# Edge keys for duplicate detection: broadcast by TensorE passes, or stored to DRAM and read back as broadcast rows

## The chip, the cores and the metric

One core of one Trainium2 chip runs the whole program. The metric is the device time of one execution in microseconds (us), as a median over runs. The engines are TensorE (PE: matmuls, and PEld: its weight loads), VectorE (DVE), ScalarE (ACT), GpSimd (POOL) and SyncE (SP), which here only issues DMAs. ScalarE and GpSimd issue DMAs too. 16 DMA engines carry the transfers of all of them.

## What is computed

The reference runs a two-layer graph network on 384 tokens of width 1024 and 12288 edges. Only the first layer's graph attention touches the edges in the part at issue:

```python
def _build_mask(edge_index, edge_type, edge_type_weights, dtype):
    src, dst = (edge_index[0], edge_index[1])
    w = jax.nn.softplus(edge_type_weights)
    mask = jnp.full((N, N), -jnp.inf, dtype=dtype)
    mask = mask.at[src, dst].set(w[edge_type - 1])     # the last edge of a (src, dst) pair wins
    ...
q = x @ wq.T + bq; k = x @ wk.T + bk; v = x @ wv.T + bv
q2, k2, v2 = second projections, 16 heads of 64
scores = einsum('hnd,hmd->hnm', q2, k2) * scale + mask[None]
out = softmax(scores) @ v2, then @ wo.T + bo
x = x + _L0_gnn_ref(xn, ...) + _L0_mix_ref(xn, ...)    # then expert layers, and layer 1
```

Layer 1 sums over the same edges and needs for each (dst, src) pair how many edges it has.

## The kernel before

**Projections on TensorE.** Six first projections of xn (three for each of two branches) are called layers 0 to 5 (`layer_A`). Each takes eight weight chunks of 512 KB from a ring of eight slots (`ring`). `chunk_T` multiplies one chunk, 8 matmuls of 384 columns, into bank 0 or 1, and ScalarE evicts it (L633). Two second projections follow (L658 evicts them), then V2 (`chunk_N`, L886) in two halves, between whose chunks the first score matmuls (L966) are written. The third score group waits until VectorE has read the first one, and VectorE reads scores only with the finished mask (L1486).

**Weights.** SyncE refills a slot each time its chunk has been used (`load`, L360).

**Edges.** 12288 edges are 96 columns of 128. An edge's key is 384 src + dst. GpSimd makes the key of each edge in a column (`keyf`) and its transpose key (`rkeyf`). To find duplicates inside a column, every partition needs all 128 keys of that column as a row. TensorE makes these rows (`keys(layer)`, L912 and L913): for each of 16 columns in a layer, two accumulating fp16 matmuls against scaled identities, into banks 4 to 7. It does so ahead of each of the six layers. VectorE's `dedup` (L1410) compares each row, read from PSUM, with its own key and counts later duplicates. It then makes scatter addresses (`kidx`, `ridx`) and counts (L1415 to L1420).

**Scatters on GpSimd.** GpSimd first fills four tables in DRAM (w_lo, w_hi, n_lo, n_hi: 576 KB each, with a tail of 0.5 KB; L471, L472). When all have landed it scatters column after column: 48 turns of four indirect DMAs (`put`, L453). A put waits for the one before it into the same table. Each group of 8 turns also waits for `spots_ready` of the dedup for one layer. Then it reads the tables back (L486), and VectorE combines them to the mask (L1464 to L1473), which the score stage needs.

**ScalarE's queue** loads the edges and constants first, and after the input transposes the two bias rows bo_g and bo_m, broadcast into `rows` (L616, L617), the gate weights wqkv and the centroids cent. GpSimd adds the two bias rows after its table reads (L496).

Of the kernel before, what the change touches and what calls it, by code (L numbers as in the profile page):

```python
# [29 lines left out]
P = 128  # L30
N = 384
# [125 lines left out]

def program(nc, x, stream, c32, c16, cols_d, edges_d, up0_d, dn0_d, wqkv_d, cent_d,
            bo_g, bo_m, a_lr, gam_d, bet_d, b2_d,
            xs, ys, yo, w_lo, w_hi, n_lo, n_hi, out):  # L160
    with ExitStack() as ctx:
        def sb(name, shape, dt=F32):
            return ctx.enter_context(nc.sbuf_tensor(name, shape, dt))

        def sem(name):
            return ctx.enter_context(nc.semaphore(name))
# [28 lines left out]
        ridx = sb("ridx", [P, ET], U32)  # L195
        src16 = sb("src16", [P, ET], F16)
        dst16 = sb("dst16", [P, ET], F16)
        wqkv = sb("wqkv", [P, KB, 3 * NE])
# [29 lines left out]
        iota = k16[:, 0:384]  # L228
        id16 = k16[:, 384:512]
        id384 = k16[:, 512:640]  # L230
        token = k16[:, 640:643]

# [40 lines left out]
        edges_ready = sem("edges_ready")  # L273
        keys_ready = sem("keys_ready")
        sp_in = sem("sp_in")
        sp_out = sem("sp_out")
# [37 lines left out]


        junk = CT[:].rearrange("p b n -> p (b n)").bitcast(BF16)[:, 0:GT_ * P].rearrange("p (t n) -> p t n", t=GT_)
        tmp = [G[:, i * 3072:(i + 1) * 3072] for i in range(3)]
# [37 lines left out]
        def _(sp):  # L355
# [3 lines left out]
            def load(r, c):  # L359
                sp.dma_start(ring[:, r, :], stream[c]).then_inc(landed[r], 16)  # L360

            for r in range(SLOTS):
                load(r, r)
            with sp.Fori(1, CH_L1 // 8) as g:
                for r in range(SLOTS):
                    sp.wait_ge(chunk_used, 8 * g - 7 + r)
                    load(r, 8 * g + r)

# [78 lines left out]
        def _(pool):  # L447
# [9 lines left out]
            step(pool.memset(none, 0.0))  # L457
            pool.wait_ge(edge_in, 16)
            pool.tensor_copy(src16[:], ed[:, 0, :])
            pool.tensor_copy(dst16[:], ed[:, 1, :]).then_inc(edges_ready, 1)  # L460
            pool.tensor_copy(srcf[:], ed[:, 0, :])
# [4 lines left out]
            pool.tensor_tensor(keyf[:], keyf[:], dstf[:], ALU.add)  # L466
            pool.tensor_tensor(rkeyf[:], rkeyf[:], srcf[:], ALU.add).then_inc(edges_ready, 1)
            pool.wait_ge(x_in[NB - 1], 16)
# [105 lines left out]
        def _(act):  # L574
            step = Chain(act, astep)
            act.dma_start(ed[:], edges_d).then_inc(edge_in, 16)
            act.dma_start(cols[:], cols_d).then_inc(k_in, 16)
# [8 lines left out]
            def seed(c):  # L586

                act.wait_ge(var_ready, c + 1)
                act.activation(lnv[:], ve[:], ACT.Sqrt).then_inc(rstd_seed, 1)
# [15 lines left out]
            step(act.activation(spw[:, 0, :], cols[:, C_EW:C_EW + 4], ACT.Copy))  # L605
            act.activation(spw[:, 2, :], spw[:, 1, :], ACT.Exp, scale=-1.0).then_inc(beta_exp, 1)
            seed(0)
            for b in range(NB):
# [6 lines left out]
            act.activation(spw[:, 1, :], spw[:, 3, :], ACT.Ln).then_inc(act_output, 1)  # L615
            act.dma_start(rows[:, 0, :], bo_g.to_broadcast([P, D])).then_inc(biases_and_gates_in, 16)  # L616
            act.dma_start(rows[:, 1, :], bo_m.to_broadcast([P, D])).then_inc(biases_and_gates_in, 16)  # L617
            act.dma_start(wqkv[:], wqkv_d).then_inc(biases_and_gates_in, 16)
# [33 lines left out]


            act.wait_ge(mixs_ready, 8)
            with act.Fori(0, 2) as j:
# [203 lines left out]
        def _(pe):  # L859
# [45 lines left out]

            def keys(layer):
                pe.wait_ge(edges_ready, 2 * layer + 2)
                for g in range(2):
                    for t in range(GT_):
                        dst = bank[4 + 2 * g + t // 4][:, (t % 4) * P:(t % 4 + 1) * P]  # L910
                        e = (layer + HG * g) * 8 + t
                        pe.matmul(dst, src16[:, bass.ds(e, 1)].to_broadcast([P, P]), id384, start=True, stop=False)  # L912
                        last = pe.matmul(dst, dst16[:, bass.ds(e, 1)].to_broadcast([P, P]), id16,  # L913
                                         start=False, stop=True)
                    last.then_inc(keys_ready, 1)

            pe.wait_ge(k_in, 48)
            keys(0)
            for b in range(NB):
# [11 lines left out]
            def layer_A(layer, before=None):  # L931
                if not isinstance(layer, int) or layer:
                    keys(layer)
                for m in range(KB):
                    if before:
                        before(m)
                    chunk_T(m, lambda k: xnT[:, k, :], layer * 8 + m + T_A - 1, layer * 16 + 16, m % 2)

            layer_A(0)
            with pe.Fori(1, 5) as layer:  # L940
                layer_A(layer)
# [58 lines left out]
            pe.wait_ge(mixs_taken, 8)  # L1000
            pe.wait_ge(edges_ready, 2 + EG)
            for kk in range(4):
# [337 lines left out]
        def _(v):  # L1340
# [62 lines left out]
            def dedup(layer, q):  # L1403

                group, turn_ = layer + HG * q, layer * 2 + q
                v.wait_ge(keys_ready, turn_ + 1)
                for t in range(GT_):
                    e = group * 8 + t
                    src = bank[4 + 2 * q + t // 4][:, (t % 4) * P:(t % 4 + 1) * P]
                    last = stt(junk[:, t, :], src, keyf[:, bass.ds(e, 1)], same, ALU.is_equal, ALU.mult,  # L1410
                               accum_out=ndup[:, bass.ds(e, 1)])
                last.then_inc(edges_ready, 1)
                v.wait_ge(edges_ready, turn_ + 3)
                g8 = bass.ds(group * 8, GT_)
                ts(count[:, g8], ndup[:, g8], 256.0, None, ALU.mult)  # L1415
                step(ts(lastf[:], ndup[:, g8], 1.0, None, ALU.is_lt))
                stt(spot[:, 0, :], keyf[:, g8], beyond, lastf[:], ALU.subtract, ALU.mult)
                step(stt(spot[:, 1, :], rkeyf[:, g8], beyond, lastf[:], ALU.subtract, ALU.mult))
                ts(kidx[:, g8], spot[:, 0, :], beyond, None, ALU.add)
                ts(ridx[:, g8], spot[:, 1, :], beyond, None, ALU.add).then_inc(spots_ready, 1)  # L1420
                v.wait_ge(spots_ready, turn_ + 1)
# [476 lines left out]
def constants():  # L1898
# [11 lines left out]
    token = np.arange(N).reshape(NB, P).T  # L1910
    c16 = np.concatenate([np.tile(np.arange(N), (P, 1)), ident, ident * N, token], 1).astype(np.float16)
    return c32, c16
# [42 lines left out]
```

## Time and profile before

| | us |
|---|---|
| median of 3 runs (1207.18 to 1212.54) | 1211.57 |
| the profiled execution, its own time | 1217.39 |
| its span in the trace | 1215.4 |
| PE busy | 1032.0 (85%) |
| DVE busy | 337.9 (28%) |
| ACT busy | 211.0 (17%) |
| POOL busy | 321.7 (26%) |

The times of this table are one execution's, apart from the median. All positions below are us from the start of its span. A share of busy time is a mean over very different stages: TensorE is busy in most of them, yet the chain of work that ended last gives 22% of the span to GpSimd. What ends each wait is to be read in the stage itself.

### The profile page before, as it was taken

The numbers are of one execution on the slowest core, as the hardware profiler recorded it, in microseconds if no ns is written. First come the engines' busy times: TensorE is split into PE (matmuls) and PEld (weight loads), VectorE is DVE, ScalarE is ACT, GpSimd is POOL, SyncE is SP. The second block draws the span as 40 slices with busy tenths as digits, with TensorE's granted clock in tenths as the row PEclk, the third lists the DMA queues.
The fourth block names the chain that finished last, engine by engine and source line by source line (L and its number), as shares of the span: only waits on it lengthen the run. The fifth ranks groups of instructions, "written<-read, shape, count | busy, mean of one in ns | idle before, by whom it ended". The sixth has DMA issues, their size and how long they took to land.

```text
span 1215.4 us, 10270 instructions
## 1 busy us (share of the span) xinstructions
PE 1032.0 (85%) x3516; PEld 562.9 (46%) x3516; DVE 337.9 (28%) x911; ACT 211.0 (17%) x443; POOL 321.7 (26%) x250
## 2 busy tenths in 40 slices
PE   6999999999999787999479997299999999357553
PEld 4566656655554344444455563144445554242210
DVE  5036332271000566110431010402204541820002
ACT  3122311111111366100111111101101000114100
POOL 3088888888888100000000000100000000002000
PEclk9999999999999899999679999599999999559777
DMA  9964544444446200122448983722230223436786
GB/s 276 165 111 95 104 92 99 92 99 88 104 104 166 102 1 1 56 85 92 147 142 296 352 325 118 272 98 98 99 104 18 87 81 96 169 111 236 284 300 246
DMA packets 62251, 170.44 MB, mean 140 GB/s; under 512 B 22144, under 2 KB 22656, under 8 KB 62080
## 3 DMA queue, kind: packets, MB, share of 16 engines
q1 hardware_dynamic: 36832, 140.53, 35.6%
q0 software_dynamic: 21632, 17.94, 8.8%
q10 hardware_dynamic: 3744, 11.42, 2.5%
q8 instruction: 24, 0.39, 0.1%
q14 instruction: 19, 0.16, 0.0%
HBM read 156.39 MB, written 13.47 MB: 140 GB/s over the span
## 4 chain that ended last, share of the span: by engine, by line
PE 49%; POOL 22%; DMA 11%; issue 8%; DVE 7%; ACT 2%; SPq 1%; ACTq 0%; DVEq 0%; POOLq 0%
PE bank L886 20%; POOL n_hi L453 7%; PE bank L1093 6%; POOL n_lo L453 6%; POOL w_hi L453 4%; POOL w_lo L453 4%; PE bank L875 3%; DMA n_hi<-G 3%; PE bank L1118 3%; PE bank L1300 2%; DMA ring<-in_stream 2%; PE bank L1318 2%; PE bank L995 1%; PE bank L981 1%; PE bank L1231 1%
## 5 line engine op out<-in xcount | busy, mean ns | idle before, releaser
L875 PE MATMUL bank<-xnT,ring 128*128 128x384 f32 x896 | 292.7, 487 | 1.5 <-ACT xnT L612 1.0
L875 PEld LDWEIGHTS bank<-xnT,ring 128*128 128x128 f32 x896 | 169.7, 190 | 119.6 <-ACT xnT L612 1.2
L506 POOL DMA_INDIRECT Y<-xs,idx x12 | 12.3, 1025 | 624.4 <-DVE idx L1603 509.5
L886 PE MATMUL bank<-ring,Y 128*128 128x512 f32 x384 | 168.5, 599 | 0.8 <-DVE Y L1820 0.8
L886 PE MATMUL bank<-ring,xnT 128*128 128x512 f32 x288 | 124.0, 592 | 0.6 <-ACT xnT L597 0.6
L886 PEld LDWEIGHTS bank<-ring,Y 128*128 128x128 f32 x384 | 73.3, 192 | 94.7 <-issue 92.5
L453 POOL DMA_INDIRECT n_hi<-count,ridx x48 | 84.4, 1758 | 14.6 <-issue 14.0
L886 PEld LDWEIGHTS bank<-ring,xnT 128*128 128x128 f32 x288 | 54.6, 190 | 68.7 <-issue 67.9
L453 POOL DMA_INDIRECT n_lo<-count,ridx x48 | 81.8, 1704 | 14.6 <-issue 14.3
L875 PE MATMUL bank<-Y,ring 128*128 x256 | 82.7, 486 | 0.0
L1093 PE MATMUL bank<-ring,Y 128*128 128x352 f32 x256 | 79.1, 468 | 0.7 <-issue 0.7
L1300 PE MATMUL bank<-ring,Y 128*64 128x512 f32 x128 | 37.3, 742 | 39.2 <-DMA ring<-in_stream 31.0
L633 ACT ACTIVATE Y<-bank,sbias,scale 128x384 f32 (+1 forms) x48 | 32.2, 671 | 214.0 <-PE bank L875 214.0
L867 PE MATMUL bank<-k,xn 128*128 128x128 f32 x72 | 17.1, 412 | 59.7 <-DVE xn L1369 58.3
L453 POOL DMA_INDIRECT w_lo<-wts,kidx x48 | 51.7, 1077 | 55.3 <-DMA n_hi<-G 40.9
L875 PEld LDWEIGHTS bank<-Y,ring 128*128 128x128 f32 x256 | 48.6, 190 | 33.9
L1093 PEld LDWEIGHTS bank<-ring,Y 128*128 128x128 f32 x256 | 49.1, 194 | 27.4 <-issue 2.6
L453 POOL DMA_INDIRECT w_hi<-wts,kidx x48 | 51.8, 1078 | 14.6 <-issue 14.6
L1410 DVE SCALAR_TENSOR_TENSOR CT<-bank,keyf,k 128x128 bf16<-128x128 f32 x96 | 27.0, 347 | 66.0 <-PE bank L913 64.6
L506 POOL DMA_INDIRECT Y<-ys,idx x9 | 8.5, 947 | 138.1 <-DMA ys<-Y 136.0
L867 PEld LDWEIGHTS bank<-k,xn 128*128 128x128 f32 x72 | 12.2, 209 | 66.4 <-DVE xn L1369 60.8
L1300 PEld LDWEIGHTS bank<-ring,Y 128*64 128x64 f32 x128 | 11.6, 169 | 62.6 <-issue 58.3
(252 smaller groups left out, 972.2 us busy)
## 6 DMA issues: line engine op xcount, KB each, us to landing
ring<-in_stream SPq DMA_DIRECT2D x160, 512.0 KB, 3.7
ring<-in_up SPq DMA_DIRECT2D x32, 704.0 KB, 5.6
G<-in_stream SPq DMA_DIRECT2D x32, 512.0 KB, 7.1
ring<-in_dn SPq DMA_DIRECT2D x7, 1024.0 KB, 5.8
ys<-Y ACTq DMA_DIRECT2D x12, 512.0 KB, 7.6
Y<-in_dn SPq DMA_DIRECT2D x7, 384.0 KB, 6.8
Y<-in_b SPq DMA_DIRECT2D x8, 256.0 KB, 11.1
xr<-in_x SPq DMA_DIRECT2D x3, 512.0 KB, 4.9
```

Source lines behind the costliest of these rows:

```text
L453: pool.indirect_dma_start(table, bass.IndirectOffsetOnAxis(ap=at[:, e:e + 1], axis=0), what[:, e:e + 1], None, **how).then_inc(done, 16)
L506: pool.indirect_dma_start(dst, None, src, bass.IndirectOffsetOnAxis(ap=idx[:, col:col + 1], axis=0))\
L633: act.activation(dst, bank[m % 2][:, 0:N], ACT.Identity, bias=bi, scale=sc).then_inc(t_evicted, 1)
L867: last = pe.transpose(bank[n % 2][:, b * P:(b + 1) * P], src[:, b, m * P:(m + 1) * P], ident)
L875: last = pe.matmul(bank[to][:, 0:N], ring[:, r, k * P:(k + 1) * P], rhs(k), start=(k == 0), stop=(k == KB - 1))
L886: last = pe.matmul(bank[2 + 3 * half + b][:], lhs(k0 + k, b), ring[:, r, k * 512:(k + 1) * 512], start=(start and k == 0), stop=(stop and ...
L981: last = pe.transpose(bank[4 + mb][:, b * P:(b + 1) * P], S[:, u, b, mb * P:(mb + 1) * P], ident)
L1093: last = pe.matmul(bank[2 + h][:, 0:F0], x_, W[:, o:o + F0], **se)
L1118: last = pe.matmul(bank[5 + half][:], h_, w_, start=(f == 0), stop=(f == 2))
L1300: last = pe.matmul(bank[2][a * HC:(a + 1) * HC, :], XgT[i % 2][:, 2 * j + k, a * HC:(a + 1) * HC], ringf[:, o:o + 512], start=(j == 0 and ...
L1318: last = pe.matmul(bank[5 + half][a * HC:(a + 1) * HC, :], hT[:, 2 * kk + k, a * HC:(a + 1) * HC], G[:, o:o + 512], start=(kk == 0 and k = ...
L1410: last = stt(junk[:, t, :], src, keyf[:, bass.ds(e, 1)], same, ALU.is_equal, ALU.mult, accum_out=ndup[:, bass.ds(e, 1)])
```

## The change

The program no longer makes the key rows on TensorE. The edges come in a second layout too (`edge_rows`, 96 partitions of 128 src and 128 dst, lying in `mask` until the mask is made). GpSimd makes a table of keys from it, 96 x 128, and ScalarE stores that to DRAM (`keys_d`, 48 KB), ahead of its first square root. SyncE then reads 8 columns at a time back, broadcast to 128 partitions, into `rows`: two reads of 512 KB for each layer, the first pair behind the eight first ring loads, the others in the middle of the layer before. VectorE's comparison reads `rows` in SBUF in place of PSUM. Since `rows` is in use, the two bias rows are loaded after layer 5. The fp16 constants and `src16`, `dst16` go.

```diff
@@ SyncE
             for r in range(SLOTS):
                 load(r, r)
-            with sp.Fori(1, CH_L1 // 8) as g:
+            def load_keys(layer):
+                for q in range(2):
+                    sp.dma_start(rows[:, q, :].rearrange("p (t n) -> p t n", t=GT_),
+                                 keys_d[bass.ds((layer + HG * q) * GT_, GT_), :].unsqueeze(0)
+                                 .to_broadcast([P, GT_, P])).then_inc(key_rows_in, 16)
+            def next_chunk(g, r):
+                sp.wait_ge(chunk_used, 8 * g - 7 + r)
+                load(r, 8 * g + r)
+            sp.wait_ge(keys_stored, 16)
+            load_keys(0)
+            with sp.Fori(1, HG) as g:
                 for r in range(SLOTS):
-                    sp.wait_ge(chunk_used, 8 * g - 7 + r)
-                    load(r, 8 * g + r)
+                    next_chunk(g, r)
+                    if r == 3:
+                        sp.wait_ge(edges_ready, 2 * g + 2)
+                        load_keys(g)
@@ GpSimd
-            pool.wait_ge(edge_in, 16)
-            pool.tensor_copy(src16[:], ed[:, 0, :])
-            pool.tensor_copy(dst16[:], ed[:, 1, :]).then_inc(edges_ready, 1)
+            pool.wait_ge(edge_in, 32)
+            pool.tensor_copy(key_row, edge_rows[:, 0, :])
+            step(pool.tensor_copy(key_dst, edge_rows[:, 1, :]))
+            step(pool.tensor_scalar(key_row, key_row, float(N), None, ALU.mult))
+            pool.tensor_tensor(key_row, key_row, key_dst, ALU.add).then_inc(keys_ready, 1)
@@ ScalarE
+            act.dma_start(edge_rows, erows_d).then_inc(edge_in, 16)
             act.dma_start(ed[:], edges_d).then_inc(edge_in, 16)
...
+            act.wait_ge(keys_ready, 1)
+            act.dma_start(keys_d, key_row).then_inc(keys_stored, 16)
             seed(0)
...
-            act.dma_start(rows[:, 0, :], bo_g.to_broadcast([P, D])).then_inc(biases_and_gates_in, 16)
-            act.dma_start(rows[:, 1, :], bo_m.to_broadcast([P, D])).then_inc(biases_and_gates_in, 16)
...
+            act.wait_ge(edges_ready, 2 + EG)
+            act.dma_start(rows[:, 0, :], bo_g.to_broadcast([P, D])).then_inc(biases_and_gates_in, 16)
+            act.dma_start(rows[:, 1, :], bo_m.to_broadcast([P, D])).then_inc(biases_and_gates_in, 16)
             act.wait_ge(mixs_ready, 8)
@@ TensorE
-            def keys(layer):
-                ...
-            keys(0)
...
             def layer_A(layer, before=None):
-                if not isinstance(layer, int) or layer:
-                    keys(layer)
@@ VectorE, dedup
-                v.wait_ge(keys_ready, turn_ + 1)
+                if q == 0:
+                    v.wait_ge(key_rows_in, 32 * layer + 32)
                 for t in range(GT_):
                     e = group * 8 + t
-                    src = bank[4 + 2 * q + t // 4][:, (t % 4) * P:(t % 4 + 1) * P]
+                    src = rows[:, q, t * P:(t + 1) * P]
                     last = stt(junk[:, t, :], src, keyf[:, bass.ds(e, 1)], same, ALU.is_equal, ALU.mult,
                                accum_out=ndup[:, bass.ds(e, 1)])
```

TensorE, head of the loop over layers. Before, the 32 key matmuls stand ahead of the 64 of a layer (the first of each kind shown; `ISA` and `REGISTER_ALU` set registers):

```order
L875 MATMUL bank<-xnT,ring 128x384 x64
L940 UNCONDITIONAL_BRANCH
L940 ISA
L912 ISA
L912 MATMUL bank<-k,src 128x128
L913 REGISTER_ALU
L913 MATMUL bank<-k,dst 128x128
```

and now:

```order
L937 MATMUL bank<-k,xn 128x128 x24
L948 UNCONDITIONAL_BRANCH
L948 ISA
L896 ISA
L898 MATMUL bank<-xnT,ring 128x384 x8
```

The layer's own matmuls now follow the transposes and each other directly, and layer 0 is inside the loop.

SyncE, start of the program and first refills. Before:

```order
L357 DMA xr<-in_x 128x1024 x3
L360 DMA ring<-in_stream 128x1024 x8
L364 UNCONDITIONAL_BRANCH
L364 ISA
L360 ISA [waits chunk_used]
L360 DMA ring<-in_stream 128x1024
```

and now (the second wait, on `edges_ready`, stands after four refills of a group):

```order
L360 DMA ring<-in_stream 128x1024 x8
L366 DMA rows<-keys 128x1024 [waits keys_stored]
L366 DMA rows<-keys 128x1024
L376 UNCONDITIONAL_BRANCH
L376 ISA
L360 ISA [waits chunk_used]
L360 DMA ring<-in_stream 128x1024
L380 ISA
L366 ISA [waits edges_ready]
L366 DMA rows<-keys 128x1024
```

Two reads of `rows` stand in front of the first refill, and two more between the fourth and the fifth refill of each of the groups 1 to 5.

VectorE, the dedup of layer 0. Before:

```order
L1397 TENSOR_TENSOR wts<-wts,ndup 128x96 [waits dstep]
L1410 SCALAR_TENSOR_TENSOR CT,ndup<-bank,keyf,k 128x128 [waits keys_ready,wts_ready]
L1410 SCALAR_TENSOR_TENSOR CT,ndup<-bank,keyf,k 128x128 x7
L1415 TENSOR_SCALAR count<-ndup 128x8 [waits edges_ready]
L1416 TENSOR_SCALAR lastf<-ndup 128x8
```

and now:

```order
L1404 TENSOR_TENSOR wts<-wts,ndup 128x96 [waits dstep]
L1418 SCALAR_TENSOR_TENSOR CT,ndup<-rows,keyf,k 128x128 [waits key_rows_in,wts_ready]
L1418 SCALAR_TENSOR_TENSOR CT,ndup<-rows,keyf,k 128x128 x7
L1423 TENSOR_SCALAR count<-ndup 128x8 [waits edges_ready]
L1424 TENSOR_SCALAR lastf<-ndup 128x8
```

Nothing moved here; the first input is `rows` in place of a PSUM bank, and the wait is for two DMAs in place of TensorE.

## Rows read from the trace of the kernel before

**Rows 1.** Chain of work that ended last: start us, us, what.

```profile
2.15 8.43 DMA k<-in_c
15.51 41.41 DMA n_hi<-G
383.46 1.58 POOL n_hi L453
387.03 9.39 DMA G<-n_hi
396.52 2.31 DVE G L1464
```

**Rows 2.** Waits of PE, 18 to 420 us: total us, times, longest us.

```profile
PE bank L966 <- DVE nmx L1486: 5.5, 1, 5.5
```

**Rows 3.** Timeline of PE, 102 to 109 us: start us, us, what.

```profile
103.38 0.22 PE L912 MATMUL bank<-k,src 128*128 128x128 f16 x1
...
105.32 4.11 PE L875 MATMUL bank<-xnT,ring 128*128 128x384 f32 x12
```

**Rows 4.** Windows: length, busy of PE, PEld, DVE, ACT, POOL, clock, DMA share, GB/s.

```profile
408.00:414.00 6.00, 6.00 (x10) 2.47 (x11) 2.72 (x14) 3.23 (x12) 0.00 (x0) 0.53 0.00 1
```

**Rows 5.** Timeline of POOL, 56 to 165 us, first scatter and one turn.

```profile
57.20 1.03 POOL L453 DMA_INDIRECT w_lo<-wts,kidx  x1 [40.95 <-DMA n_hi<-G]
...
114.06 0.99 POOL L453 DMA_INDIRECT w_lo<-wts,kidx  x1 [0.30 <-issue]
...
120.44 0.99 POOL L453 DMA_INDIRECT w_lo<-wts,kidx  x1 [0.30 <-issue]
```

**Rows 6.** DMA issues, whole span and four windows: KB each, us to landing.

```profile
rows<-in_bo_m ACTq DMA_DIRECT2D x1, 512.0 KB, 31.3
n_hi<-G POOLq DMA_DIRECT2D x1, 0.5 KB, 41.4
...
ring<-in_stream SPq DMA_DIRECT2D x1, 512.0 KB, 32.3
...
ring<-in_stream SPq DMA_DIRECT2D x1, 512.0 KB, 23.9
...
ring<-in_stream SPq DMA_DIRECT2D x1, 512.0 KB, 22.6
...
ring<-in_stream SPq DMA_DIRECT2D x3, 512.0 KB, 4.5
```

**Rows 7.** Windows of the start, columns as in Rows 4.

```profile
20.00:28.00 8.00, 8.00 (x27) 4.69 (x26) 7.38 (x45) 0.67 (x1) 0.00 (x0) 1.00 0.84 58
28.00:30.00 2.00, 2.00 (x8) 1.21 (x7) 1.43 (x10) 0.67 (x1) 0.00 (x0) 1.00 1.09 417
30.00:38.00 8.00, 8.00 (x27) 4.69 (x26) 0.00 (x0) 0.67 (x1) 0.00 (x0) 1.00 0.99 63
38.00:41.00 3.00, 3.00 (x11) 1.81 (x10) 0.00 (x0) 0.67 (x1) 0.00 (x0) 1.00 1.02 414
41.00:49.00 8.00, 8.00 (x27) 4.69 (x26) 0.00 (x0) 0.67 (x1) 0.00 (x0) 1.00 1.01 112
```

**Rows 8.** Timeline of DVE, first and last instruction of the dedup of layer 0.

```profile
22.82 0.35 DVE L1410 SCALAR_TENSOR_TENSOR CT<-bank,keyf,k 128x128 bf16<-128x128 f32 x1
...
29.31 0.22 DVE L1420 TENSOR_SCALAR ridx<-spot,k 128x8 uint32<-128x8 f32 x1
```

**Rows 9.** POOL's stretched scatters, and DVE beside them, by timelines.

```profile
60.94 3.36 DVE L1434 SCALAR_TENSOR_TENSOR G<-Y 128x3072 f32 x1 [31.41 <-ACT Y L633]
...
61.77 3.98 POOL L453 DMA_INDIRECT n_hi<-count,ridx  x1 [0.30 <-issue]
66.06 0.99 POOL L453 DMA_INDIRECT w_lo<-wts,kidx  x1 [0.30 <-issue]
...
268.14 0.56 DVE L1457 TENSOR_TENSOR Y<-Y,G 128x384 f32<-128x384 f32 x1
268.20 1.95 POOL L453 DMA_INDIRECT n_hi<-count,ridx  x1 [0.30 <-issue]
```

**Rows 10.** Line L1410: ns min/median/max, and two neighbours on DVE's timeline.

```profile
L1410 DVE SCALAR_TENSOR_TENSOR CT<-bank,keyf,k x96: 341/347/352, 22.8 to 240.3; 128x128 bf16<-128x128 f32 x96
...
65.58 0.34 DVE L1410 SCALAR_TENSOR_TENSOR CT<-bank,keyf,k 128x128 bf16<-128x128 f32 x1
65.85 0.34 DVE L1410 SCALAR_TENSOR_TENSOR CT<-bank,keyf,k 128x128 bf16<-128x128 f32 x1
```

More of the change, by code:

```diff
@@ L155, in leave, with program @@
         self.n, self.off = self.mark + self.per * turns, 0
-def program(nc, x, stream, c32, c16, cols_d, edges_d, up0_d, dn0_d, wqkv_d, cent_d,
+def program(nc, x, stream, c32, c16, cols_d, edges_d, erows_d, up0_d, dn0_d, wqkv_d, cent_d,
             bo_g, bo_m, a_lr, gam_d, bet_d, b2_d,
-            xs, ys, yo, w_lo, w_hi, n_lo, n_hi, out):
+            xs, ys, yo, keys_d, w_lo, w_hi, n_lo, n_hi, out):
     with ExitStack() as ctx:
@@ L195, in program @@
         ridx = sb("ridx", [P, ET], U32)
-        src16 = sb("src16", [P, ET], F16)
-        dst16 = sb("dst16", [P, ET], F16)
         wqkv = sb("wqkv", [P, KB, 3 * NE])
@@ L228, in program @@
         iota = k16[:, 0:384]
-        id16 = k16[:, 384:512]
-        id384 = k16[:, 512:640]
-        token = k16[:, 640:643]
+        token = k16[:, 384:387]
         def YT(s):
@@ L274, in program @@
         keys_ready = sem("keys_ready")
+        keys_stored = sem("keys_stored")
+        key_rows_in = sem("key_rows_in")
         sp_in = sem("sp_in")
@@ L312, in program @@
         stored = sem("stored")
+        edge_rows = mask[0:ET, 0, 0:2 * P].bitcast(I32).rearrange("p (a n) -> p a n", a=2)
+        key_row, key_dst = mask[0:ET, 1, 0:P], mask[0:ET, 1, P:2 * P]
         junk = CT[:].rearrange("p b n -> p (b n)").bitcast(BF16)[:, 0:GT_ * P].rearrange("p (t n) -> p t n", t=GT_)
@@ L363, in _ @@
                 load(r, r)
-            with sp.Fori(1, CH_L1 // 8) as g:
-                for r in range(SLOTS):
-                    sp.wait_ge(chunk_used, 8 * g - 7 + r)
-                    load(r, 8 * g + r)
+            def load_keys(layer):
[9 more added lines that the diff above has]
+            with sp.Fori(1, HG) as g:
+                for r in range(SLOTS):
+                    next_chunk(g, r)
+                    if r == 3:
+                        sp.wait_ge(edges_ready, 2 * g + 2)
+                        load_keys(g)
+            with sp.Fori(HG, CH_L1 // 8) as g:
+                for r in range(SLOTS):
+                    next_chunk(g, r)
             def load_up(e, j):
@@ L466, in _ @@
             pool.tensor_tensor(keyf[:], keyf[:], dstf[:], ALU.add)
-            pool.tensor_tensor(rkeyf[:], rkeyf[:], srcf[:], ALU.add).then_inc(edges_ready, 1)
+            pool.tensor_tensor(rkeyf[:], rkeyf[:], srcf[:], ALU.add).then_inc(edges_ready, 2)
             pool.wait_ge(x_in[NB - 1], 16)
@@ L904, in xtok @@
                 return xnT[:, k, b * P:(b + 1) * P]
-            def keys(layer):
[L907 to L915, printed above, removed]
             pe.wait_ge(k_in, 48)
-            keys(0)
             for b in range(NB):
@@ L937, in layer_A @@
                     chunk_T(m, lambda k: xnT[:, k, :], layer * 8 + m + T_A - 1, layer * 16 + 16, m % 2)
-            layer_A(0)
-            with pe.Fori(1, 5) as layer:
+            with pe.Fori(0, 5) as layer:
                 layer_A(layer)
@@ L1000, in _ @@
             pe.wait_ge(mixs_taken, 8)
-            pe.wait_ge(edges_ready, 2 + EG)
             for kk in range(4):
@@ L1910, in constants @@
     token = np.arange(N).reshape(NB, P).T
-    c16 = np.concatenate([np.tile(np.arange(N), (P, 1)), ident, ident * N, token], 1).astype(np.float16)
+    c16 = np.concatenate([np.tile(np.arange(N), (P, 1)), token], 1).astype(np.float16)
     return c32, c16
@@ L1932 @@
         "x": I["x"], "stream": weight_stream(I), "c32": c32, "c16": c16, "cols": cols, "edges": edges,
+        "edge_rows": np.stack([I[n].reshape(ET, P) for n in ("src", "dst")], 1),
         "up0": I["L0_ffn_w1"].transpose(0, 2, 1).reshape(NE, 4, 2, P, 2 * F0).transpose(0, 1, 3, 2, 4)
@@ L1948 @@
         args.append(nc.dram_tensor(name, (n, D), F32, kind="Internal").ap())
+    args.append(nc.dram_tensor("keys", (ET, P), F32, kind="Internal").ap())
     for name in ("w_lo", "w_hi", "n_lo", "n_hi"):
```

## The prediction

> **What bounds the kernel now.** I read the chain of waits first, then the waits of TensorE in the first third, then the timelines of GpSimd and VectorE there, and last the landings of the DMAs. The reader is to see in the chain that the first 396 us belong to the mask and not to the projections: the constants land at 10.6, the table fills at 56.9 (15.51 + 41.41), then GpSimd scatters until 385.0 (383.46 + 1.58), the tables are back at 396.4, and VectorE starts the mask [rows 1]. TensorE, busy for nearly all of that time, is ahead of it. From 18 to 420 us it waits for VectorE once, 5.5 us, at the third group of scores [rows 2], which needs the mask. So the program reaches the attention stage when GpSimd's chain lets it, and 5.5 us of TensorE's work are already given away there.
>
> GpSimd's chain has three terms. Its start, 57.20, is set by the fill landings [rows 5]. A turn of four scatters takes 120.44 - 114.06 = 6.38 us where nothing disturbs it [rows 5], and 48 turns are 306.2. From 57.20 to 385.04 it took 327.8, so 21.6 us are stretched scatters: one has 3.98 us beside a 3.36 us VectorE instruction with SBUF inputs, where undisturbed scatters of its kind, such as the last in the chain, have 1.58 [rows 1, 9].
>
> **TensorE's key passes go.** A pass ahead of a layer lasts from 103.38 to 105.32, 1.94 us [rows 3], and stands ahead of layers 1 to 5: 5 x 1.94 = 9.7 us. The pass of layer 0 lies before the transposes, where TensorE waits for the input anyway. So TensorE reaches the third score group 9.7 us earlier and finds no mask: the wait grows from 5.5 to 15.2 us. Worth at the end: 0. What is late next is what is late now, the mask. TensorE's clock after the wait is already at the lower level before (0.53 granted over 408 to 414 [rows 4], close to 1.2 of 2.4 GHz), so a longer wait has little left to take; I price it at 0, bounds 0 and +3 (half of those 6 us again).
>
> **The start of the scatters.** Four things act on it. (1) ScalarE's queue has one more issue ahead of the constants, whose landing at 10.6 releases the fills [rows 1]; edge_rows is 96 KB and the fp16 constants shrink by 64 KB. I take +0.4 us, bounds 0 and +1. (2) ScalarE waits for GpSimd's keys ahead of the square root, and issues the store; this delays the normalised input and with it TensorE, which has 15 us to spare, and nothing else. (3) Two bias broadcasts, 1 MB, leave the time before 57 us and two key reads, 1 MB, come into it. The DMA engines are full there: bursts of over 400 GB/s (28 to 30, 38 to 41) stand between stretches of 8 us with 58, 63 and 112 GB/s at nearly the same busy share [rows 7]. What makes these slow stretches the trace doesn't tell. As the bytes are the same I take 0, bounds -8 and +8, one slow stretch more or less. (4) The first scatter now also needs the dedup of layer 0, and that the key rows. The dedup takes 29.53 - 22.82 = 6.7 us [rows 8]. To be ready at 57.2, the second key read must land by 50.5. SyncE issues both at about 16, behind the eighth ring load, which was issued at 5.9 and landed at 38.2 (32.3 us [rows 6]). The next load in that queue, issued at 24.1, landed at 48.0 (23.9), the one after two more, issued at 34.4, at 57.0 (22.6). The bias broadcast on the other queue, issued at 18.0, landed at 49.3 (31.3 [rows 6]). The key reads take the place of the first refills and no longer share with the bias rows. Bounds for the second: 39 and 57. I take 48, from the refill in whose place they stand and the bias row of the same size and kind. The dedup is then done at 54.7, 2.5 us ahead of need. Term: 0, bounds 0 and +6.5.
>
> **SyncE's refills** stand behind the key reads. Its second pair waits for the dedup of layer 0, so the four refills after it are issued at about 55 in place of 44.6 and later. TensorE needs the first of them at about 80; with some 5 to 10 us to land that is hidden. From layer 2 on, a dedup is over long before the middle of its layer. TensorE has 15 us of cover in all; without it these terms would count.
>
> **The comparisons read SBUF.** Sixteen of them stand in each layer, 0.35 us each at a pitch of 0.27 [rows 10], and those of layers 1 to 5, ten bursts of eight and 2.2 us each, run beside the scatters. Before, one input came from PSUM; the scatter of 66.06, which began while such a burst was running (65.85 [rows 10]), took its normal 0.99 [rows 9]. Now both streaming inputs lie in SBUF. Two instructions of that form bound the price: beside 3.36 us the scatter that began at 61.77 ended 1.45 us after VectorE's 64.30, that is 2.4 over its normal 1.58; beside 0.56 us the scatter that began 0.06 later took 1.95, 0.37 more [rows 1, 9]. So a scatter waits until the running instruction ends. With 0.35 us instructions that is 0.1 to 0.3 for each scatter that starts in a burst; one or two do, in ten bursts: 1 to 6 us. Lowest is 0 (no hit). Highest is a scatter that is kept out to the burst's end, about 1.4 us in each of ten: 14. I take +2, from the row of 0.56, the nearest in size.
>
> The Trainium skill (SBUF — State Buffer, section "Who interferes with whom") says that a VectorE instruction with two SBUF inputs contends with a GpSimd instruction that reads SBUF and that the second to issue blocks until the first is finished. By that rule the trace's 3.98 us is what one expects, and the change adds contention where there was none; whether the next VectorE instruction of a burst gets in ahead of a waiting scatter the page does not say. It would give a slower kernel by my second or first case.
>
> **The table reads.** At 385 to 396 TensorE is 9.7 us further on, and parked. Of the three ring loads issued from 384 to 400 [rows 6] two would then be gone from beside the four table reads (9.39 us for the last [rows 1]). 1 MB at 400 GB/s is 2.6 us. I take -1, bounds -3 and 0. The bias rows are loaded after layer 5, at about 270, and needed after 387: hidden.
>
> **Sum.** 0 (TensorE) + 0.4 + 0 + 0 + 2 - 1 = +1.4 us on the profiled execution's own 1217.39 (span 1215.4): 1218.8. That execution lies 5.8 above the median of the runs shown, 1211.57; against the median it is 1213.0. Half a per cent, about what a measurement of this kernel can tell from no change, is 6 us.
>
> **The rivals.**
> - *Bursts lock the scatters out* (slower, the other side of no change). Instructions at a pitch shorter than their length [rows 10] leave no gap, so a waiting scatter gets in only behind the eighth. For it: length over pitch. Against it: 3.36 us instructions one after another let one scatter in between each, though each of those waits for a semaphore first. Price 14 in place of 2: 1225. It decides if scatters of 2.5 us and more stand beside the comparisons.
> - *The key rows are late* (slower). The second read lands as late as the third refill did, 57.0; dedup until 63.7, scatters start 6.5 later: 1219.5. It decides from a landing after 50.5.
> - *The fills get a larger share* (faster). Without the bias rows ScalarE's queue is nearly empty, two queues share the DMA engines in place of three, and one slow stretch falls away: fills in at 49, and the key rows before 43 as well. -7: 1206. Against it: both have to come early, and the key reads bring the same bytes. The Trainium skill (DMA: Bandwidth & Descriptors, section "SWDGE vs HWDGE vs iDMA") has each DMA engine alternate between its queues, GpSimd's and the others' being different ones; that speaks for this case, and no row of this trace shows it by itself.
> - *TensorE sets the pace after all*: then the 9.7 us are saved, 1203. The 5.5 us wait [rows 2] speaks against it.
>
> **How the numbers follow.** Forecast 0.58, lock-out 0.15, late rows 0.12, larger share 0.12, TensorE 0.03. Late rows and lock-out are over the bound of 6: slower 0.27. Larger share is over it in three quarters, with TensorE: faster 0.12. Same: 0.61. The forecast's own range is 1208 to 1219 (its small terms at their bounds, and the 5 us between the runs shown). The whole range, with fills and lock-out near their ends, is 1205 to 1226.
>
> **What would show it.** Right: no key matmuls; TensorE's wait at the third score group near 15 us; first scatter at 55 to 60; scatters for 328 to 332 us; the chain through GpSimd's scatters as before. Wrong: a scatter start outside 50 to 63, with the last release by the dedup and not by the fills (key rows late); scatters together over 338 us (lock-out); a wait of TensorE for a ring load before 385. If the wait at the scores doesn't grow, my reading of the bound has failed.

## The result: half a per cent slower, through the same chain

The changed kernel takes 1215.16 us (median of 13 runs, 1211.55 to 1222.22) against 1209.51 for the kernel before on the same chip (13 runs, 1206.78 to 1214.04): ratio 1.0054, 95% interval 1.0033 to 1.0075. Timed a second time (after_third below) it is 1.0034, 1.0017 to 1.0051. The difference is 4 to 6 us, where 1.4 were forecast. The first lies just under the 6 us at which the prediction set its bound between no change and slower; both are inside the forecast's own range. Two timed executions that came out far longer, 1667.95 us of pin_before and 2269.82 us of the kernel before in one session, are in no ratio.

The profiled execution after has 1221.51 us of its own, 1219.7 span. Its chain of work that ended last (start us, us, what):

```profile
2.71 9.36 DMA k<-in_c
...
19.32 26.11 DMA rows<-keys
...
169.82 5.54 DMA w_lo<-wts,kidx
276.21 7.68 DMA n_lo<-count,ridx
385.21 9.30 DMA G<-n_hi
...
1128.90 16.97 DMA ring<-in_stream
```

This answers to [rows 1]. The mask is the end of the first third as before, and it hangs on the scatters. Two things are new. The 41.41 us of the fills are gone from the chain; the store of the key table and the key rows' 26.11 us stand in their place. And at two landings of scatters, the links at 169.82 and 276.21, GpSimd now stands idle. (The chain before has such a link too, 4.20 us from 327.89, but GpSimd idles only the usual 0.30 us there.)

The store is issued late. GpSimd has the key table ready at 8.30, but ScalarE's issue stands behind its wait for the constants, which land at 12.07. From the timelines of GpSimd and of ScalarE's queue:

```profile
7.85 0.45 POOL L479 TENSOR_TENSOR mask<-mask 96x128 f32<-96x128 f32 x1
...
12.53 0.35 ACTq L628 DMA_DIRECT2D keys<-mask  x1
```

So about 4 us of the chain are the place of one issue in ScalarE's program. No run here moved it, and whether the reads would then land as much earlier isn't shown.

GpSimd's timeline, the first scatter, then one and the next into the same table, and the last (answers to [rows 5]):

```profile
53.15 1.03 POOL L470 DMA_INDIRECT w_lo<-wts,kidx  x1 [35.24 <-DVE ridx L1428]
...
276.21 1.62 POOL L470 DMA_INDIRECT n_lo<-count,ridx  x1 [0.30 <-issue]
...
284.15 1.61 POOL L470 DMA_INDIRECT n_lo<-count,ridx  x1 [1.87 <-DMA n_lo<-count,ridx]
...
381.81 1.58 POOL L470 DMA_INDIRECT n_hi<-count,ridx  x1 [0.30 <-issue]
```

The first scatter is released by VectorE (L1428, the end of a dedup) and no longer by the last fill. The scatter at 284.15 waits 1.87 us until its predecessor into the same table, issued at 276.21, has landed. The other gap is 1.42 us long, ahead of a scatter into n_hi at 175.44. The profile puts it down to the landing of w_lo (169.82), but in the program that scatter waits for its own table's predecessor, which GpSimd issued at 167.94, some 7.5 us before. What streams beside the two landings the timelines of the queues tell, SyncE's and ScalarE's:

```profile
168.30 0.88 SPq L366 DMA_DIRECT2D rows<-keys  x2
...
276.19 0.34 ACTq L675 DMA_DIRECT2D rows<-in_bo_g  x1
```

The first is a pair of key reads, the second the first of the two bias rows in their new place; each pair is 1 MB. VectorE's timeline shows what the dedup itself waited for, and its end:

```profile
45.54 0.35 DVE L1418 SCALAR_TENSOR_TENSOR CT<-rows,keyf,k 128x128 bf16<-128x128 f32 x1 [18.81 <-DMA rows<-keys]
...
52.06 0.23 DVE L1428 TENSOR_SCALAR ridx<-spot,k 128x8 uint32<-128x8 f32 x1
```

The DMA landings before 30 us, of the page's kind (KB each, us to landing):

```profile
keys<-mask ACTq DMA_DIRECT2D x1, 48.0 KB, 6.4
...
n_hi<-G POOLq DMA_DIRECT2D x1, 0.5 KB, 28.8
```

The last fill needed 28.8 us where it had 41.4 [rows 6], and was in at 46.0, 6.3 us before the dedup was done (52.29). In after_again and after_third the fills were in at 52.5 and 44.9, the dedup was done at 53.9 and 50.5. So in all three the key rows hold the start. The key store took 6.4. The waits of TensorE from 14 to 425 us (total us, times, longest us), which answer to [rows 2]:

```profile
PE bank L937 <- DVE xn L1376: 16.5, 1, 16.5
PE bank L974 <- DVE nmx L1494: 9.7, 1, 9.7
```

TensorE starts at 16.5, and its wait at the third score group has grown from 5.5 to 9.7. Saved matmuls became waiting.

One line of this profile isn't the change's. Behind the last scatter's end it has 1221.51 - 383.39 = 838.1 us, and before had 832.4. Of these 5.7 us about 4 lie after 1080 us, the most of it in loads of the ring such as that of 1128.90, 16.97 us, in the last expert stage. Two more executions of the same program have 831.7 and 830.7 there.

### The profile page after: what moved, and what is told of

It reads as the page before. It is cut to its first block, busy times and chain, and to the rows that moved or that the text cites. A ratio compares the mean times of both kernels' runs of the same rounds, so it can differ in the third digit from the quotient of the medians.

```text
span 1219.7 us, 9803 instructions
## 1 busy us (share of the span) xinstructions
PE 1020.8 (84%) x3324; PEld 553.3 (45%) x3324; DVE 338.6 (28%) x911; ACT 211.5 (17%) x443; POOL 322.6 (26%) x252
## 4 chain that ended last, share of the span: by engine, by line
PE 47%; POOL 22%; DMA 12%; issue 8%; DVE 8%; ACT 2%; SPq 1%; ACTq 0%; DVEq 0%; POOLq 0%
PE bank L909 20%; POOL n_lo L470 7%; PE bank L1100 6%; POOL n_hi L470 6%; POOL w_lo L470 4%; POOL w_hi L470 4%; PE bank L898 3%; PE bank L1125 3%; DMA ring<-in_stream 3%; DMA rows<-keys 2%; PE bank L1307 2%; PE bank L1325 2%; PE bank L1003 1%; PE bank L890 1%; PE bank L1238 1%
## 5 line engine op out<-in xcount | busy, mean ns | idle before, releaser
L470 POOL DMA_INDIRECT n_lo<-count,ridx x48 | 84.4, 1757 | 16.2 <-issue 14.3
L470 POOL DMA_INDIRECT n_hi<-count,ridx x48 | 79.4, 1655 | 15.7 <-issue 14.3
L1418 DVE SCALAR_TENSOR_TENSOR CT<-rows,keyf,k 128x128 bf16<-128x128 f32 x96 | 27.2, 349 | 65.4 <-DMA rows<-keys 64.5
## 6 DMA issues: line engine op xcount, KB each, us to landing
Y<-in_b SPq DMA_DIRECT2D x8, 256.0 KB, 11.5
```

The lines of the kernel that those rows point to most:

```text
L470: pool.indirect_dma_start(table, bass.IndirectOffsetOnAxis(ap=at[:, e:e + 1], axis=0), what[:, e:e + 1], None, **how).then_inc(done, 16)
```

## The experiments

**One measure for all.** For each profiled execution I take its own time less the end of its last scatter. Over 14 executions of ten programs it is 828.5 to 832.6 but for the 838.1 above. So, for these kernels, the time is the end of the last scatter plus 831 us, give or take 2.5, and the table shows where an end comes from. "Gaps" is GpSimd's idle time between scatters beyond the 0.3 us that stands ahead of each; nearly all of it is waiting for the landing of an earlier scatter.

| execution | first scatter | released by | end of last | from first to end | gaps | ratio of runs to before |
|---|---|---|---|---|---|---|
| before | 57.20 | fills | 385.04 | 327.8 | 0 | |
| before_again | 56.91 | fills | 384.89 | 328.0 | 0.2 | |
| before_third | 47.69 | fills | 376.70 | 329.0 | 0.7 | |
| dram_layout | 50.83 | fills | 378.99 | 328.2 | 0 | 0.9987 (0.9970 to 1.0004) |
| bias_late | 52.01 | fills | 380.00 | 328.0 | 0.9 | 0.9988 (0.9961 to 1.0015) |
| after | 53.15 | dedup | 383.39 | 330.2 | 2.7 | 1.0054 (1.0033 to 1.0075) |
| after_again | 54.77 | dedup | 386.16 | 331.4 | 3.9 | |
| after_third | 51.39 | dedup | 382.70 | 331.3 | 3.4 | 1.0034 (1.0017 to 1.0051) |
| pe_first | 45.64 | fills | 376.33 | 330.7 | 2.3 | 0.9988 (0.9963 to 1.0014) |
| pin_before | 62.28 | TensorE | 391.75 | 329.5 | 0 | 1.0082 (1.0057 to 1.0107) |
| pin_after | 65.58 | TensorE | 399.07 | 333.5 | 4.7 | 1.0150 (1.0124 to 1.0176) |
| reads_twice | 52.54 | dedup | 391.22 | 338.7 | 12.2 | 1.0124 (1.0096 to 1.0151) |
| early_before | 30.28 | dedup | 380.42 | 350.1 | 22.4 | 1.0025 (0.9998 to 1.0051) |
| early_pe_first | 34.13 | dedup | 376.03 | 341.9 | 15.4 | 0.9993 (0.9973 to 1.0014) |

Each ratio is taken against runs of the kernel before in the same session, so two rows are compared by way of the kernel before. The theory to be tested: the slower time comes from GpSimd's chain alone, from the first read of key rows, which now holds the start of the scatters, and from waits between scatters while the broadcast rows stream. Rivals: the comparisons lock the scatters out; something off the chain (where the data lie in DRAM, the moved bias rows).

**before_again and before_third** (the kernel before, unchanged), **after_again and after_third** (the changed kernel, unchanged). What they ask is how far one execution's start can be trusted.

> The kernel before, once more, for a second profile of it. Its first profiled execution (1217.4) lay 8 us above the median of its 13 timed runs (1209.5). Theory A (a floor under the start): most executions of the kernel before have their table fills in well before 56.9 us, so this one starts its scatters at 47 to 52 us and its span is 1206 to 1212. Theory B (something late in the program differs, by the placement of tensors in DRAM or by chance in the weight loads of the last stage): the first scatter is at 57 again, within 2 us.

> The kernel before, a third profile. Theory A2: its fill landing, and so its first scatter, varies between executions from 50 to 58 us (57.2 and 56.9 so far; 50.8 in dram_layout, which runs the same instructions), and its own time is 829 to 833 us behind the last scatter whatever the start.

> The changed kernel, once more, for a second profile. Theory A: the first scatter is released by VectorE's dedup and not by the fills, at 50 to 55 us, and the scatters have some 3 us of waits for the DMA of the scatter before them, beside the key reads and the bias rows. Theory B: scatter start varies with the fills; up to 1080 us it is level with the kernel before, and lies 3 to 6 us behind only after 1110.

> The changed kernel, timed again and profiled a third time. Theory A2: 1.003 to 1.008 of the kernel before; first scatter released by the dedup at 52 to 56, scatter waits of 2 to 5 us, last scatter at 382 to 387, own time 829 to 833 us behind it. If the loss were in the last stage (the first profile of the changed kernel has 838 there, all others 829 to 833), it shows 836 or more again.

GpSimd's first scatter in before_again:

```profile
56.91 1.03 POOL L453 DMA_INDIRECT w_lo<-wts,kidx  x1 [40.40 <-DMA n_hi<-G]
```

and first and last in before_third:

```profile
47.69 1.03 POOL L453 DMA_INDIRECT w_lo<-wts,kidx  x1 [30.98 <-DMA n_hi<-G]
...
375.12 1.58 POOL L453 DMA_INDIRECT n_hi<-count,ridx  x1 [0.30 <-issue]
```

The same program, the same release, 9.2 us apart, and the last scatter follows it: 383.31 in before_again, 375.12 here. The first came where the rival had it, the second earlier than the 50 to 58 expected. The changed kernel's two, first after_again, then after_third:

```profile
54.77 1.03 POOL L470 DMA_INDIRECT w_lo<-wts,kidx  x1 [36.95 <-DVE ridx L1428]
```

```profile
51.39 1.03 POOL L470 DMA_INDIRECT w_lo<-wts,kidx  x1 [33.34 <-DVE ridx L1428]
```

Both are released by VectorE, as expected, and all three of this kernel lie within 3.4 us. Over five executions with the start of the kernel before (bias_late and dram_layout included) the first scatter varies by 9.5. In before_third, dram_layout and bias_late TensorE has no wait at the place of [rows 2]: the 5.5 us are an execution's, not the kernel's, and where the fills are early TensorE and the mask arrive at nearly the same time.

**dram_layout** is the kernel before with one more input and one more DRAM tensor, both unused, so that its instructions are the old ones:

```
+        "edge_rows": np.stack([I[n].reshape(ET, P) for n in ("src", "dst")], 1),
+    args.append(nc.dram_tensor("keys", (ET, P), F32, kind="Internal").ap())
```

> The kernel before with the two new DRAM tensors (96 KB and 48 KB) declared and not used, so that all other tensors lie where they do in the changed kernel. Theory B (placement in DRAM): 4 to 7 us slower than the kernel before. Theories A and A2: within 2 us of it.

```profile
50.83 1.03 POOL L453 DMA_INDIRECT w_lo<-wts,kidx  x1 [34.11 <-DMA n_hi<-G]
```

0.9987: the two new tensors cost nothing that can be told, and this rival falls. (The changed kernel's fp16 constants are 64 KB smaller too; that part of the layout is not copied here.)

**bias_late** is the kernel before with the two bias broadcasts behind layer 5, as in the changed one, and nothing else:

```
-            act.dma_start(rows[:, 0, :], bo_g.to_broadcast([P, D])) ...
-            act.dma_start(rows[:, 1, :], bo_m.to_broadcast([P, D])) ...
...
+            act.dma_start(rows[:, 0, :], bo_g.to_broadcast([P, D])) ...
+            act.dma_start(rows[:, 1, :], bo_m.to_broadcast([P, D])) ...
             act.wait_ge(mixs_ready, 8)
```

> The kernel before with one part of the change alone: the two bias rows are loaded after layer 5. Theory A: fills in earlier, first scatter at 40 to 48 us; TensorE, which had 5 us to spare, limits the gain: 2 to 6 us faster than the kernel before, less what one scatter waits beside the bias rows (2 us). Theory B: same as the kernel before, within 2 us.

```profile
52.01 1.03 POOL L453 DMA_INDIRECT w_lo<-wts,kidx  x1 [35.57 <-DMA n_hi<-G]
```

The first scatter is inside the spread of the kernel before, the ratio 0.9988 with 1 inside its interval. So 1 MB less beside the fills is worth nothing that can be told, where 2 to 6 us were expected. The late place costs the chain one gap of 0.9 us, at 289.07, when the bias rows have been issued, too little for the runs to tell.

**pe_first** is the changed kernel, but the key rows of layer 0 come from TensorE as before, VectorE reads them from PSUM, and SyncE reads none at the start. Key rows of layers 1 to 5 are read from DRAM:

```
-            load_keys(0)
...
+            pe.wait_ge(keys_ready, 2)
+            for g in range(2):
+                for t in range(GT_):
...
+                    pe.matmul(dst, src16[:, e:e + 1].to_broadcast([P, P]), id384, start=True, stop=False)
+                    last = pe.matmul(dst, dst16[:, e:e + 1].to_broadcast([P, P]), id16, start=False, stop=True)
+                last.then_inc(key_rows_in, 16)
```

> The changed kernel with the key rows of layer 0 made by TensorE as before (beside its wait for the input) and no key read at the start; layers 1 to 5 read from DRAM. Theory A: dedup of layer 0 over at about 31 us, fills in at 40 to 48 because neither bias rows nor key rows share the DMA engines, first scatter at 41 to 48: 5 to 10 us faster than the changed kernel, 0 to 5 us faster than the kernel before. Theory B: as slow as the changed kernel, within 2 us.

```profile
45.64 1.03 POOL L473 DMA_INDIRECT w_lo<-wts,kidx  x1 [27.45 <-DMA n_hi<-G]
...
374.75 1.58 POOL L473 DMA_INDIRECT n_hi<-count,ridx  x1 [0.30 <-issue]
```

The dedup of layer 0 is done at 31.47, the fills release again, and the ratio is back at 0.9988. Against the changed kernel that is 0.46 to 0.66%, 5.6 to 8 us (each uncertain by about 4), inside the 5 to 10 expected. By the runs the first read of key rows is thus the larger part of the loss. From first to last scatter it still has 330.7, 2.5 more than the 328.2 that the first five rows have on average: that part isn't in the start.

**pin_before and pin_after** hold the first scatter in both kernels until TensorE has used its eighth chunk of weights, so that neither fills nor dedup release it:

```
             pool.wait_ge(wts_ready, 1)
+            pool.wait_ge(chunk_used, 8)
```

> The kernel before with one more wait ahead of the first scatter: for the eighth weight chunk to be used, which comes at 59.8 us by TensorE's own pace and not by the DMAs. In both profiles of the kernel before the first scatter is at 57, yet pe_first, which starts them 11 us earlier in its profile, was timed only 1 to 3 us faster. Theory A2 (in executions without the profiler the fills of the kernel before land earlier than in the profiled ones, so that the true start is 50 to 53): 6 to 9 us slower than the kernel before. Theory B2 (the start is 57 in the timed executions too, and the changed kernel loses its time elsewhere): 2 to 4 us slower.

> The changed kernel with the same wait. Its layer 0 ends some 2 us later, so the first scatter is at about 61.8 in place of 53 to 55. Theory A2: 7 to 9 us slower than the changed kernel, and slower than pin_before by the 2 us of the later start and the 3 us of waits beside the key reads and bias rows: 4 to 6 us. Theory B2: pin_after is 8 us or more above pin_before, since the loss is neither the start nor those waits.

First scatter of pin_before, then of pin_after:

```profile
62.28 4.21 POOL L453 DMA_INDIRECT w_lo<-wts,kidx  x1 [45.56 <-PE bank L876]
```

```profile
65.58 4.21 POOL L470 DMA_INDIRECT w_lo<-wts,kidx  x1 [47.37 <-PE bank L899]
```

The pin didn't equalise the starts, since TensorE itself is 3.3 us later there. It does show the chain's price: pin_before starts 9.4 us later than the mean of the five free starts (52.9), and its runs are 0.82%, 9.9 us, slower, just over the 6 to 9 expected. And it shows the second part apart: 333.5 against 329.5 us from first scatter to end, 4.0 more with the start taken out. The runs of pin_after are 0.68% above those of pin_before, 8.2 us. I had expected 4 to 6 from the start and the waits, and 8 or more if the loss lay elsewhere, so by that test the theory missed. The traces answer it in part: the last scatter ends 7.3 us later, 3.3 by the start, where 2 were expected, and 4.0 between the scatters, where 3 were. The last 1 us of the 8.2 is within the uncertainty of the two ratios. Of TensorE's passes nothing is seen: in pin_after TensorE waits 24.8 us for the mask, in pin_before 10.9.

**reads_twice** is the changed kernel with each key read of layers 1 to 5 made a second time, into an area of Y that is not in use then, and the dedup waits for both (ScalarE also waits for the last of them before it evicts layer 5 there):

```
+            for q, into in [(q, rows[:, q, :]) for q in range(2)] + \
+                    [(q, Y[:, 5, q * D:(q + 1) * D]) for q in range(2) if twice]:
...
-                        load_keys(g)
+                        load_keys(g, True)
```

> The changed kernel with each key read of layers 1 to 5 done twice, the second copy into an unused area, 5 MB more in all. In the two profiles of the changed kernel scatters waited 2.7 and 3.9 us for the DMA of the scatter before them; the kernel before has 0 and 0.2. If the key reads and bias rows cause that, it rises by 2 to 6 us here, and the kernel is as much slower than the changed one. If the transfers don't matter: the same as the changed kernel, within 1 us.

GpSimd's waits up to 400 us in reads_twice (total us, times, longest us):

```profile
POOL n_lo L471 <- DMA n_lo<-count,ridx: 8.3, 5, 2.7
...
POOL w_lo L471 <- DMA w_lo<-wts,kidx: 3.4, 3, 1.5
POOL n_hi L471 <- DMA n_hi<-count,ridx: 3.2, 2, 1.7
```

and the same view of the changed kernel:

```profile
POOL n_lo L470 <- DMA n_lo<-count,ridx: 1.9, 1, 1.9
POOL n_hi L470 <- DMA w_lo<-wts,kidx: 1.4, 1, 1.4
```

The comparisons are the same 96 in both, the reads are doubled, and the gaps go from 2.7 (2.7 to 3.9 over three executions) to 12.2. From first to last scatter it is 338.7 in place of 330.2 to 331.4, and the runs are 0.7 to 0.9% slower than the changed kernel's, 8 to 11 us. That is more than the 2 to 6 expected, and the same way. So it is the streaming of broadcast rows, not the comparisons, that holds scatters back (11.0 of the 12.2 come within 14 us of the issue of key reads, 1.2 behind the bias rows; in the changed kernel's three executions it is 1.1, 2.9 and 1.3 near key reads and 1.6, 1.0 and 2.0 near the bias rows): it delays the landing of a scatter beyond one turn, and the next into that table waits.

**early_before and early_pe_first** were to take the start out. Each table's first scatter waits for its own fill alone, and the scatters of the w tables run three turns ahead of those of the n tables; the first is done to the kernel before, the second to pe_first, which also tells the worth of TensorE's passes where the mask comes early.

```
-                if n:
-                    pool.wait_ge(done, 16 * n)
+                pool.wait_ge(done, 16 * n + 32)
...
+            AHEAD = 3
+            for i in range(ET // 2 + AHEAD):
```

> The kernel before (key passes on TensorE) with the scatter chain made shorter: each put waits for the fill of its own table alone, and the scatters into the two w tables run three turns ahead of those into the two n tables. The chain then ends some 10 us earlier. Theory A2 (the chain through GpSimd ends at 379 to 381 in a typical execution of the kernel before, and TensorE reaches the scores at about 400): TensorE becomes the bound; 0 to 3 us faster than before. Rival (the chain's end decides alone and TensorE's passes are worth nothing): 8 to 10 us faster.

> The same shorter scatter chain in pe_first, where TensorE makes the key rows of layer 0 alone. Theory A2: the chain ends at about 368 us, TensorE reaches the scores at 393 and is the bound: 7 to 11 us faster than the kernel before, and 6 to 9 us faster than early_before, the worth of the five passes that go (9.7 us) once the chain does not hide it. Rival: as early_before, within 2 us.

GpSimd's first scatter in early_before:

```profile
30.28 1.03 POOL L452 DMA_INDIRECT w_lo<-wts,kidx  x1 [14.20 <-DVE ridx L1422]
```

and its longest wait for a scatter's landing:

```profile
POOL w_lo L452 <- DMA w_lo<-wts,kidx: 17.9, 3, 14.2
```

and the same of early_pe_first, on the timeline:

```profile
44.48 0.96 POOL L472 DMA_INDIRECT w_lo<-wts,kidx  x1 [8.01 <-DMA w_lo<-wts,kidx]
```

I had counted on ends some 10 us earlier. The scatters began at 30.3 and 34.1 and ended at 380.42 and 376.03, about where the kernel before ends too (376.70 to 385.04): in the crowded start the second scatter into a table waits 14.2 or 8.0 us for the first one's landing, and the gaps total 22.4 (3.7 of it for a fill) and 15.4. TensorE still waits for the mask, 2.0 and 2.5 us, so the passes never came to count, and the two ratios overlap. The question of their worth with an early mask stays open. Neither version beats the kernel before measurably; nor does any other here.

## Why the prediction was right, and which terms were off

The mechanism was named right: the mask ends the first third, GpSimd's scatters bring it, TensorE's savings are given away. The size was not: +1.4 forecast, 4 to 6 measured, and the two terms that make the difference, the dedup as a floor under the start and the waits between scatters, stood at nothing in the sum. That the time still fell inside the range is partly luck, since the range was made for other things.

- **TensorE's key passes: 0, as forecast.** TensorE's wait for the mask is 9.7, 13.5 and 9.8 in the three executions, not 15.2. In the first, the mask came 1.9 us earlier (394.62 against 396.52), and TensorE began layer 0 at 22.76 in place of 18.52, 4.2 later: 15.2 - 1.9 - 4.2 = 9.1, near the 9.7. Of the 4.2, 1.8 are its start. The rest is a use of the pass of layer 0 that the prediction missed when it set it beside the wait for the input: the 24 transposes behind it run slower without it. Before, and now:

```profile
14.73 2.84 PE L926 MATMUL bank<-k,xn 128*128 128x128 f32 x24 [0.52 <-DVE xn L1369]
```

```profile
16.48 5.30 PE L937 MATMUL bank<-k,xn 128*128 128x128 f32 x24 [16.48 <-DVE xn L1376]
```

In pe_first, where the pass is back, they take 2.84 again. The granted clock is shown as 1.00 in all three, so the rows don't tell why. It costs nothing here, since TensorE waits later. One limit: in the early executions of the kernel before TensorE has no slack left, so the passes may be worth a little there. Own time less the last scatter's end is 831.1 to 832.6 in those three and 829.5 in pe_first, which is too near to tell.
- **TensorE's clock: 0, as forecast.** Over 408 to 414 us the granted clock is 0.77 where it was 0.53 [rows 4]; the wait, though longer, ends earlier (406.28 against 407.93), and the low stretch behind it is no longer than before:

```profile
408.00:414.00 6.00, 6.00 (x11) 2.63 (x12) 1.85 (x9) 1.58 (x6) 0.00 (x0) 0.77 0.00 0
```
- **The constants** landed at 12.07 (2.71 + 9.36), 1.5 later than 10.6; forecast +0.4, bounds 0 to 1. Missed, and it counts: the store of the key table stands behind them, and it is the store and the key reads that now hold the start.
- **The key rows: mis-sized only in what they stand against.** Landing 45.4 against 48 forecast, dedup done at 52.3 against 54.7, and 53.9 and 50.5 in the other two. That is right within its bounds, though the reads were issued at 19, not 16. The step that failed is "2.5 us ahead of need": the need was read from [rows 5] of one execution, 57.20, and that is the latest of five (47.69 to 57.20). The fills themselves came in at 46 in the changed kernel, about as the rival with the larger share said, and this gained nothing, since the dedup is a floor under the start. The kernel before can start at 48; the changed one cannot before its key rows are in. The gain of pe_first shows it.
- **Waits between scatters: the term that was missing.** A landing that lags behind a turn of 6.38 us [rows 5] costs what it lags. The prediction called the bias rows hidden in their new place, and weighed what the key reads do to the start and to SyncE's refills, not to the small scatters beside them. Mean from first scatter to end is 331.0 for the changed kernel and 328.2 for the first five rows of the table: +2.8, near the gaps of 2.7 to 3.9. This stands inside "328 to 332", by another cause than the one I gave.
- **The comparisons from SBUF: +2 forecast, under 0.5 measured.** GpSimd's and VectorE's timelines of the changed kernel:

```profile
178.70 0.98 POOL L470 DMA_INDIRECT w_hi<-wts,kidx  x1 [0.31 <-issue]
179.99 1.70 POOL L470 DMA_INDIRECT n_lo<-count,ridx  x1 [0.30 <-issue]
```

```profile
179.85 0.35 DVE L1418 SCALAR_TENSOR_TENSOR CT<-rows,keyf,k 128x128 bf16<-128x128 f32 x1
...
180.13 0.35 DVE L1418 SCALAR_TENSOR_TENSOR CT<-rows,keyf,k 128x128 bf16<-128x128 f32 x1
```

The scatter of 179.99 begins 0.14 us into one comparison of a burst of eight, and takes 1.70 where undisturbed ones have 1.62 (276.21). Such hits cost 0.03 to 0.11 each, five, two and five of them in the three executions. It gets in between them: the rival of a lock-out to the burst's end is false. The stretch of all scatters over their undisturbed length is 21.1 to 21.5 us in the three executions, against 21.0 to 22.2 in the five with the start of the kernel before. The Trainium skill's rule (SBUF — State Buffer, section "Who interferes with whom") holds in kind for the 3.36 us instructions, beside which a scatter of 1.58 took 3.98 [rows 9]; for short ones the trace shows next to nothing.
- **The table reads: -1 forecast, 0 measured.** From the end of the last scatter to the mask's start it takes 11.2, 11.3 and 11.7 us, against 11.5 (396.52 - 385.04), 11.0 and 12.5 before.
- **SyncE's refills: hidden, as forecast.** TensorE waits for no ring load before the scores.
- **The late stages** don't move: 831 us behind the last scatter in both.

Together the profiled executions give +0.2 for the mean start (53.1 against 52.9) and +2.8 for the scatters, 3.0 of the 4 to 6 us. Their starts vary by up to 9.5 us, so the share of the start isn't settled by them; the runs of pe_first, 5.6 to 8 us faster with only the first read gone, put more of it there. How often the kernel before starts early in executions that are not profiled can't be seen.

## What to carry to other kernels

A chain that starts behind DMAs in a crowded start has a different length in each execution: take two or three profiles before counting slack against it, and treat a second prerequisite at nearly the same time as a cost, because it cuts off the early executions. Before moving work from an engine onto the DMA queues, list the small transfers that wait one for the other there; big reads beside them delay their landings, and those may be the critical path. Work saved on an engine that waits later, here 9.7 us of matmuls, becomes waiting.

## What the runs showed of the hardware that was not expected

The same fills, with the same instructions around them, released the first scatter at 57.2, 56.9, 50.8 and 47.7 us. Stretches at full DMA share and a low rate [rows 7] differ between executions: from 30 to 38 us the three of the kernel before move 63, 125 and 190 GB/s at a share of 0.99, 1.15 and 0.93. From 20 to 28 us, before_again and before_third move 59 and 87 GB/s (length; busy of PE, PEld, DVE, ACT, POOL; clock, DMA share, GB/s):

```profile
20.00:28.00 8.00, 8.00 (x27) 4.69 (x26) 7.13 (x43) 0.90 (x3) 0.00 (x0) 1.00 1.11 59
```

```profile
20.00:28.00 8.00, 8.00 (x26) 4.75 (x25) 6.93 (x41) 1.10 (x3) 0.00 (x0) 1.00 1.02 87
```

and the changed kernel, without the bias rows there, more (113 and 117 in its other two executions):

```profile
20.00:28.00 8.00, 7.03 (x25) 4.59 (x24) 2.34 (x10) 3.28 (x5) 0.00 (x0) 1.00 1.02 147
```

It isn't the bias rows as such, since bias_late has 69 there. What makes these stretches slow was not found. And a small indirect scatter, which usually lands within a turn of 6.38 us, took 7.68 us beside the bias rows (276.21) and longer in the start: the second into its table began at 44.48 in early_pe_first, released by the landing of the one of 34.13, some 10 us; in early_before at 50.43, some 20 us after 30.28:

```profile
50.43 0.96 POOL L452 DMA_INDIRECT w_lo<-wts,kidx  x1 [14.16 <-DMA w_lo<-wts,kidx]
```
